# A streamed residual with gathered weights: loads in groups of four batches, stores in groups of five

## The reference

```python
x: (64, 128, 2048) float32      # batches B, channels C, time T
itok_B_0_15: (64,) int32        # a state 0..15 for each batch
weights: (16, 128, 128) float32 # states, C, D

W = weights[itok_B_0_15]
x = x + einsum('bct,bcd->bdt', x, W)
```

## Time and profile before

| | |
|---|---|
| median of 3 runs | 320.03 us (319.14 to 320.74) |
| profiled execution | 318.97 us, span 317.5 us |
| PE matmul busy | 250.2 us (79%), 512 instructions |
| DVE busy | 146.8 us (46%) |
| POOL busy | 18.9 us (6%) |
| DMA | 4892 packets, 135.29 MB, mean 426 GB/s over the span |
| granted TensorE clock | mean 0.894 |

### The profile page before, as it was taken

One profiled execution on the slowest core, in us unless ns is written; L12 is line 12 of the kernel. 1 busy time (PEld: TensorE's weight loads), 2 busy tenths in 40 slices (PEclk: granted clock), 3 DMA queues, 4 the chain that ended last, 5 costly groups with the idle time before them and its releaser, 6 DMA issues.

```text
span 317.5 us, 1341 instructions
## 1 busy us (share of the span) xinstructions
PE 250.2 (79%) x512; PEld 106.2 (33%) x512; DVE 146.8 (46%) x65; POOL 18.9 (6%) x69
## 2 busy tenths in 40 slices
PE   0099999999949699795987969689597995959900
PEld 0044444444424244242433424234242442424400
DVE  0026676577525616265371554717247352552620
POOL 0001000100100100000000000000000010000000
PEclk9999999999969969799795989979789798986965
DMA  8999999999999999999999999999999999999997
GB/s 330 405 454 413 400 438 425 433 427 429 446 417 454 421 442 429 429 438 421 450 417 454 421 438 425 433 433 429 446 425 442 425 433 429 429 442 425 450 417 327
DMA packets 4892, 135.29 MB, mean 426 GB/s; under 512 B 538, under 2 KB 666, under 8 KB 666
## 3 DMA queue, kind: packets, MB, share of 16 engines
q1 hardware_dynamic: 2584, 68.29, 50.4%
q10 hardware_dynamic: 2306, 66.98, 48.9%
HBM read 68.16 MB, written 67.11 MB: 426 GB/s over the span
## 4 chain that ended last, share of the span: by engine, by line
DMA 72%; PE 21%; DVE 3%; issue 0%; SPq 0%
DMA out<-x_ring 38%; DMA x_ring<-x 34%; PE product L106 21%; DVE x_ring L127 3%; SPq L58 0%
## 5 line engine op out<-in xcount | busy, mean ns | idle before, releaser
L106 PE MATMUL product<-x_ring,chosen_weights 128*128 128x512 f32 x512 | 250.2, 653 | 51.8 <-DMA x_ring<-x 51.8
L127 DVE TENSOR_TENSOR x_ring<-product,x_ring 128x2048 f32<-128x2048 f32 x64 | 146.7, 2292 | 155.5 <-PE product L106 155.5
L106 PEld LDWEIGHTS product<-x_ring,chosen_weights 128*128 128x128 f32 x512 | 106.2, 210 | 195.0 <-issue 125.4
L90 POOL COPY chosen_weights<-weight_table 128x128 f32 x64 | 18.7, 293 | 278.7 <-DVE x_ring L127 271.4
L120 DVE TENSOR_SCALAR state_row<-condition_row 1x64 int32<-1x64 int32 x1 | 0.2, 182 | 2.0 <-DMA condition_row<-condition 2.0
L167 POOL MEMSET const-float32-0.0<- 128x1 f32 x1 | 0.1, 98 | 0.1
L167 POOL MEMSET const-bfloat16-1.0<- 128x1 bf16 x1 | 0.1, 101 | 0.0
L167 POOL MEMSET const-uint8-127<- 128x1 uint8 x1 | 0.1, 101 | 0.0
L167 POOL MEMSET const-float32-1.0<- 128x1 f32 x1 | 0.1, 98 | 0.0
L167 POOL BASE_LOAD x1 | 0.0, 17 | 0.1
## 6 DMA issues: line engine op xcount, KB each, us to landing
x_ring<-x SPq DMA_DIRECT2D x16, 4096.0 KB, 30.9
out<-x_ring ACTq DMA_DIRECT2D x15, 4096.0 KB, 44.6
out<-x_ring ACTq DMA_DIRECT2D x1, 3968.0 KB
weight_table<-weights SPq DMA_DIRECT2D x1, 1024.0 KB, 5.0
out<-x_ring SPq DMA_DIRECT2D x1, 124.0 KB
condition_row<-condition ACTq DMA_DIRECT2D x1, 0.2 KB
out<-x_ring SPq DMA_DIRECT2D x1, 4.0 KB
```

The lines of the kernel that those rows point to most:

```text
L90: pool.tensor_copy(chosen_weights[b % WEIGHT_SLOTS][:, :], weight_table[:, bass.ds(state[b] * features, features)]).then_inc(weights_chose ...
L106: last = pe.matmul(product[:, b % psum_slots, m * BANK_COLUMNS:(m + 1) * BANK_COLUMNS], chosen_weights[b % WEIGHT_SLOTS][:, :], x_ring[:, ...
L127: dve.tensor_tensor(tile, product[:, b % psum_slots, :], tile, AluOpType.add).then_inc(sum_done[b], 1)
```

## The change

Loads stay in groups of four batches. Stores go in groups of five: 12 stores of 128 rows of 40 KB and one last store of four batches (32 KB rows, less the narrow strip, which is stored as before). The ring keeps its 20 batches: it has five places for loads and four for stores. A load of batches b to b+3 overwrites batches b-20 to b-17, which lie in one or two stores, and waits for each of them. A store waits for the sum of its last batch. PE waits at every fourth batch as before. x and out are passed flat, group after group, and the host reorders out by groups of five. The work of PE, DVE and POOL is the same.

Which stores a load waits for follows from `stored_for`:

| load | batches | waits for stores |
|---|---|---|
| 5 | 20-23 | 0 |
| 6 | 24-27 | 0, 1 |
| 7 | 28-31 | 1, 2 |
| 8 | 32-35 | 2, 3 |
| 9 | 36-39 | 3 |
| 10 | 40-43 | 4 |
| 11 | 44-47 | 4, 5 |
| 12 | 48-51 | 5, 6 |
| 13 | 52-55 | 6, 7 |
| 14 | 56-59 | 7 |
| 15 | 60-63 | 8 |

```diff
-GROUP = 4
-ROOMS = 5
+RING = 20
+LOAD = 4
+STORE = 5
...
+def groups_of(batches, size):
+
+    return [(b, min(b + size, batches)) for b in range(0, batches, size)]
...
+    loads, stores = groups_of(batches, LOAD), groups_of(batches, STORE)
+    load_rooms, store_rooms = RING // LOAD, RING // STORE
+
+    def rows(flat, first, end):
+        start, columns = first * channels * time, (end - first) * time
+        return flat[start:start + channels * columns].rearrange("(c t) -> c t", c=channels)
+
+    def stored_for(first, end):
+
+        return range((first - RING) // STORE, (end - 1 - RING) // STORE + 1)
...
-                for g in range(groups):
-                    room = g % ROOMS
-                    if g >= ROOMS:
-                        sp.wait_ge(room_stored[room], 16 * (g // ROOMS))
-                    sp.dma_start(x_ring[:, room * group_columns:(room + 1) * group_columns], x[g]
-                                 ).then_inc(x_loaded[g % ROOMS], 16)
...
+                for g, (first, end) in enumerate(loads):
+                    if first >= RING:
+                        for s in stored_for(first, end):
+                            sp.wait_ge(room_stored[s % store_rooms], 16 * (s // store_rooms + 1))
+                    b = first % RING
+                    sp.dma_start(x_ring[:, b * time:(b + end - first) * time], rows(x, first, end)
+                                 ).then_inc(x_loaded[g % load_rooms], 16)
...
-                for g in range(groups - 1):
-                    room, last = g % ROOMS, (g % ROOMS + 1) * GROUP - 1
-                    act.wait_ge(sum_done[last], sums_wanted(g // ROOMS, last))
-                    act.dma_start(out[g], x_ring[:, room * group_columns:(room + 1) * group_columns]
-                                  ).then_inc(room_stored[room], 16)
...
+                for s, (first, end) in enumerate(stores):
+                    turn, last = divmod(end - 1, RING)
+                    act.wait_ge(sum_done[last], sums_wanted(turn, last))
+                    target = rows(out, first, end)
+
+                    width = target.shape[1] - (time // 8 if end == batches else 0)
+                    column = first % RING * time
+                    act.dma_start(target[:, 0:width], x_ring[:, column:column + width]
+                                  ).then_inc(room_stored[s % store_rooms], 16)
```

More of the change, by code:

```diff
@@ L30, in sem @@
             return ctx.enter_context(nc.semaphore(name))
-        x_ring = sbuf("x_ring", [channels, ROOMS * group_columns])
+        x_ring = sbuf("x_ring", [channels, RING * time])
         weight_table = sbuf("weight_table", [channels, states * features])
@@ L137, in _ @@
                               ).then_inc(condition_loaded, 16)
-                for g in range(groups - 1):
-                    room, last = g % ROOMS, (g % ROOMS + 1) * GROUP - 1
-                    act.wait_ge(sum_done[last], sums_wanted(g // ROOMS, last))
-                    act.dma_start(out[g], x_ring[:, room * group_columns:(room + 1) * group_columns]
[L142 to L152, removed]
+                for s, (first, end) in enumerate(stores):
+                    turn, last = divmod(end - 1, RING)
+                    act.wait_ge(sum_done[last], sums_wanted(turn, last))
+                    target = rows(out, first, end)
+                    width = target.shape[1] - (time // 8 if end == batches else 0)
+                    column = first % RING * time
+                    act.dma_start(target[:, 0:width], x_ring[:, column:column + width]
+                                  ).then_inc(room_stored[s % store_rooms], 16)
+                for r in range(store_rooms):
+                    if r != (len(stores) - 1) % store_rooms:
+                        act.wait_ge(room_stored[r], 16 * len(range(r, len(stores), store_rooms)))
         def end_of_stores(act):
-            room = (groups - 1) % ROOMS
-            act.wait_ge(room_stored[room], 16 * (len(range(room, groups, ROOMS)) + 2))
+            room = (len(stores) - 1) % store_rooms
+            act.wait_ge(room_stored[room], 16 * (len(range(room, len(stores), store_rooms)) + 2))
         end_of_stores(nc.scalar)
@@ L168, with flat @@
     batches, channels, time = x.shape
-    grouped = np.asarray(x).reshape(batches // GROUP, GROUP, channels, time).transpose(0, 2, 1, 3)
+    def flat(a, size):
+        return np.concatenate([a[first:end].transpose(1, 0, 2).reshape(-1)
+                               for first, end in groups_of(batches, size)])
     arrays = {
-        "x": np.ascontiguousarray(grouped).reshape(batches // GROUP, channels, GROUP * time),
+        "x": flat(np.asarray(x), LOAD),
         "condition": np.ascontiguousarray(itok_B_0_15),
@@ L177 @@
     out = nc.dram_tensor("out", arrays["x"].shape, mybir.dt.float32, kind="ExternalOutput").ap()
-    conditioned_residual(nc, *args, out)
+    conditioned_residual(nc, *args, out, batches, time)
     result = run_bass_kernel_spmd(nc, [arrays], core_ids=[0])
-    grouped = result.results[0]["out"].reshape(batches // GROUP, channels, GROUP, time)
-    return np.ascontiguousarray(grouped.transpose(0, 2, 1, 3)).reshape(batches, channels, time)
+    returned = result.results[0]["out"]
+    parts = []
+    for first, end in groups_of(batches, STORE):
+        part = returned[first * channels * time:end * channels * time]
+        parts.append(part.reshape(channels, end - first, time).transpose(1, 0, 2))
+    return np.ascontiguousarray(np.concatenate(parts))
```

33 lines of the change are left out of this document (16 added, 17 removed).

## The result

The changed kernel takes 337.9 us, the median of six runs (332.9 to 342.1); the kernel before takes 319.56 us beside it (319.06 to 320.74). The ratio is 1.048, with an interval of 1.045 to 1.051. The runs of this kernel spread by 9 us (in a second series from 330.2 to 341.9), the ratio rests on the three fastest of the six, and both of its profiled executions, 339.9 and 340.6 us, are among the longest, so the traces show the loss at its larger end. By the medians the loss is some 18 us, by the ratio 15.

A forecast was written before the change was run, and what follows sets the result against it. The prediction took the full DMA engines (433 GB/s) as the bound. To the 320.0 us median it added a 6.8 us hole before the last store and −0.2 us for fewer rows: 326.6 us, range 319.8 to 329.5.

The forecast's parts named there:

- The turns go by rows: DMA engines alternate queues row by row, 1.52 us per store row against 1.21 per load row, so the store backlog drains.
- Longer rows: Fewer, longer store rows save a fixed price of about 8 ns a row, 24 rows per engine: −0.2 us.
- issues: Three store issues fewer on ACT, 0.34 us each, hidden behind its waits: no effect.
- the late first store: First store issued at 38.2 us instead of 34.77, covered by queued loads: no cost, 3.4 us without that cover.
- P: Work of stores outstanding when load 15 lands: 12.9 us instead of 22.9, bounds 10.6 to 16.7.
- the hole: DMA engines empty before the last store: 18.7+1.0−12.9 = 6.8 us, bounds 2.4 to 9.7.
- Each turn of a load lets a store's row through, so about all three are gone when load 15 lands: Stores 8 to 10, 24 rows at 1.52 us, drain beside loads 13 to 15; half a row, 0.8 us, taken as left.
- hardly starts before: Store 11 is issued 2.5 to 3.7 us before load 15 lands, so its whole 12.1 us is still outstanding then.
- rival E: A second hole mid-run when load 9 or 13 meets empty queues, some 5 us: 331.6 us; chance 0.05.
- The rule on whole transfers as one turn: An engine drains a transfer's 8 rows as one turn: hole 7.6 us or none, the latter given chance 0.01.
- rival C: Turns even out by bytes, so load and store share engine time equally: hole 3.3 us, 323.1 us median; chance 0.04.

The follow-up runs named there:

- e4: The changed kernel mirrored: loads in groups of five batches (40 KB rows), stores in groups of four (32 KB rows); 319.29 us, ratio 1.0002 to the kernel before.
- e9: The changed kernel with every load and store cut into four transfers, load rows of 8 KB and store rows of 10 KB; 330.78 us, ratio 1.035.
- e10: Control for e9: the kernel before, groups of four on both sides, every load and store cut into four transfers of 8 KB rows; 323.58 us, ratio 1.014.
- e8: The changed kernel with stores of four batches for the first 40 batches, then four stores of five and a last of four; 326.56 us, ratio 1.021.
- e11: The kernel before, groups of four and 32 KB rows on both sides, with a ring of 16 batches instead of 20; 325.39 us, ratio 1.019.
- e17: The changed kernel with the addition over the first 256 of 2048 columns only, all matmuls kept; 341.78 us.
- e7: The changed kernel with its last two stores issued as four, of 3, 2, 2 and 2 batches; 336.58 us (328.92 to 342.74).
- e6: The changed kernel with the 40 KB rows of its stores 48 KB apart in out instead of 40 KB; 337.22 us.
- e5: The kernel before with its 32 KB rows 40 KB apart in out; 319.33 us, ratio 0.9994.
- e12: New kernel of two streams, nothing computed: 16 loads in 32 KB rows into two rooms, 13 stores in 40 KB rows of a constant room; 316.18 us.
- e14: As e13, but with 16 stores in 32 KB rows; 316.74 us.
- e16: The two streams of e13 with matmuls and additions of the real sizes beside them, out still a constant; device time 336.2 us.
- e18: The changed kernel with one matmul of four and the addition over 512 of 2048 columns; 323.18 us, ratio 1.013.
- e13: As e12, but each store waits until the load after the one beside it has landed, so the store queue runs dry and restarts; 317.01 us.
- e1: The changed kernel run again, unchanged, for a second record; 337.16 us, ratio 1.040 to the kernel before.

## Why the prediction was wrong

*Direction and mechanism: right.* Slower was forecast with 0.85. The turns go by rows, loads land 21.8 us apart beside stores, the middle runs near the old rate up to 240 us, the loss is in holes before the last stores, and double waits cost nothing in e4. Longer rows, issues and the late first store were put at 0.2 us or nothing; no run measures them alone.

*The term that was mis-sized: P, and with it the hole.* The prediction put the landing of the last load at 295 us, P at 12.9 and one hole of 6.8. The record has 306.6 us, P of 7.9 on most engines, and two holes of 8.2 and 11.9. Taken apart on the chip, the mechanism is worth about what was forecast: 7.2 us with short rows (e9 against e10), 7.3 with four long stores (e8), 6.1 with a group less of ring (e11, by its own sum 6.5). The failed step is the one that took a row of a store as 1.52 us on all engines, all the way: "Each turn of a load lets a store's row through, so about all three are gone when load 15 lands". For stores 8 to 10 five engines needed 1.9 to 2.5 us for most rows. These engines fell behind the rest by up to 15 us, and each wait is for all 16. Ten engines had done load 15 by 293.2 us, before the 295 of the forecast; the landing came at 306.6. Loads 14 and 15 took 50.4 us after load 13 instead of 43.7. So loads 13 to 15 landed late, the other engines ran out of rows twice, and nothing brought the time back. The step "hardly starts before", of store 11, went with it: the store was issued 5.1 us before the late landing instead of 2.5 to 3.7, found no load rows beside it on most engines, and 4.2 us of it were gone.

*A bound that was too narrow.* The range's upper end came from P alone. A second hole stood in rival E, with 0.05, as a stop in the middle; it came at the end. The hole before the store ahead of the last is the same mechanism, one store earlier, and the prediction did not ask for it.

*What is shown and what is not.* That engines fall behind, and that the landings wait for them, is read from the completions in each record. That this is a cost of its own is supported by e9: with long rows some 18 us, with short rows 7.2. But shorter rows change the grain of the turns as well, and the count of slow rows does not measure the cost: e17 has 66 and the longest time, e7 has 112 and a run of 328.9 us. In e6 and e17 one engine behind was enough. What makes an engine's store rows slow is open. Not enough by itself, each by its run: the distance of rows in memory (e5, e6), a wait for two stores (e4), unequal rows or a queue that restarts (e12 to e14), PE and DVE beside such streams (e16), VectorE's writes (e17). 40 KB store rows were slow in numbers only in the real ring with all its matmuls and long stores all the way; in e18, with a quarter of the matmuls, and in e8, with four long stores, none was. In both records of the changed kernel most of the slow engines are out of step with the majority (they start a store's row while the others are in a load's), and they are slow only while both queues have work. That is no more than a coincidence seen: at least one slow engine was in step at 240 us, one that was out of step was not slow, and e13 and e16 have engines out of step with hardly a slow row.

*The rule on whole transfers as one turn.* By the Trainium skill, DMA: Bandwidth & Descriptors, section "Queues, rings and completion order", eight rows of a transfer would have gone as one turn. The records of single packets after the change show load and store rows in turn one by one wherever both queues have rows, on most engines at 1.21 and 1.51 us; the trace does not agree. The 4 KB packet on which rival C drew stands in the Trainium skill, DMA: Bandwidth & Descriptors, section "SWDGE vs HWDGE vs iDMA", in the account of the descriptors that GpSimd writes. The transfers here are issued by SP and ACT, and a row of 40 KB is one packet.

## What to carry to other kernels

With two full queues an engine took a row of each in turn here, so the longer row got the larger share. Find out which queue's backlog covers the end of the kernel, and keep its rows no longer than the other's: loads by five and stores by four were free, the reverse cost 15 to 18 us. Compare the work outstanding at the last landing with the time from that landing to the last store; here it was 22.9 against 19.3 us, and 3.7 us of margin was all that an otherwise full kernel had. A transfer is as late as its slowest engine. Look at the spread of its 16 completions and not only at the mean rate: in e17 15 were there by 289.7 us and the last at 312.3.

## What the runs showed of the hardware

- Rows of one size are not of one duration: in the changed kernel, from 240 to 290 us, a 40 KB row took 1.51 us on eleven engines and mostly 1.9 to 2.5 us on the other five; in e1 it was six engines, in e17 one, from 184 us on.
- A queue that starts beside a full one costs: in the kernel before, the last two load rows of an engine ahead of the first store's took up to 2.6 us instead of 1.21, and the store issued at 34.77 us had its first row at 39.5. In e6 and e17 load rows were slow in the same way from 236 to 241 us, just before the store queue started again.
- Short rows cost more than forecast: 8 KB rows on both sides cost 4.2 us (e10), at 427 GB/s instead of 433 from 88 to 280 us.
